# Delta rule in chunks: the odd heads on exchanged halves of the rows, and the last scan piece between the two halves of the per-chunk products

## The reference

```python
H, CHUNK = 4, 64
h = silu(causal_conv4(x));  q, k = l2norm(h @ Wq), l2norm(h @ Wk);  v = h @ Wv   # per head
beta = sigmoid(h @ Wb);  g = h @ Wg
def step(S, xs):                       # over the chunks of one head
    qc, kc, vc, bc = xs
    kb = kc * bc[:, None]
    A = jnp.tril(kb @ kc.T, -1)
    U = solve_triangular(eye + A, vc * bc[:, None] - kb @ S, lower=True)
    o = qc @ S + jnp.tril(qc @ kc.T) @ U
    return (S + kc.T @ U, o)
out = (rms_norm(o) * norm_w * silu(g)) @ Wo
```

## Time and profile before

| | us |
|---|---|
| median of 3 runs (823.71 to 824.50) | 824.07 |
| span of the profiled execution | 869.1 |
| in it: until the delta stage | 113.6 |
| in it: delta stage, steps 2 to 15 | 144.3 |
| in it: what follows the delta stage | 579.8 |

### The profile page before, as it was taken

The page is one execution under the profiler, slowest core; times in us unless marked ns, Lnnn a source line. Parts: engine busy times, 40 slices in busy tenths (PEclk is TensorE's granted clock), DMA queues, the critical chain, the costliest instruction groups (busy, mean ns, idle before and its releaser), DMA issues. The chain is left out here.

```text
span 869.1 us, 38511 instructions
## 1 busy us (share of the span) xinstructions
PE 638.0 (73%) x15559; PEld 550.7 (63%) x15559; DVE 388.2 (45%) x1166; ACT 275.3 (32%) x666; POOL 375.3 (43%) x773
## 2 busy tenths in 40 slices
PE   5775457888888585616998368889985269989993
PEld 4564346888888484516988335567664158978992
DVE  3664602222222135661666413445762844456662
ACT  4552211111111121404665133434532023334441
POOL 4574554211110372055888473220100444387675
PEclk9796655555555566856999757889997569999997
DMA  4001231131110470064655110000000556555551
GB/s 124 8 15 32 69 91 40 59 97 49 54 49 34 142 225 1 0 105 144 196 181 171 40 43 23 16 15 4 4 4 2 91 140 203 191 182 184 198 192 38
DMA packets 64818, 75.08 MB, mean 86 GB/s; under 512 B 16048, under 2 KB 42704, under 8 KB 64704
## 3 DMA queue, kind: packets, MB, share of 16 engines
q1 hardware_dynamic: 60384, 64.38, 24.1%
q0 software_dynamic: 4320, 9.18, 4.4%
HBM read 19.83 MB, written 11.24 MB: 36 GB/s over the span
## 5 line engine op out<-in xcount | busy, mean ns | idle before, releaser
L2017 PE MATMUL e_psH<-spare,e_up_w 128*128 x728 | 102.2, 284 | 9.7 <-issue 6.2
L2017 PEld LDWEIGHTS e_psH<-spare,e_up_w 128*128 128x128 f32 x728 | 90.1, 195 | 18.1 <-issue 18.1
L586 POOL TENSOR_TENSOR tb<-tinv,mb 128x128 f32<-128x128 f32 x64 | 24.3, 403 | 116.3 <-PE d_psY L606 110.1
L2082 ACT ACTIVATE e_pre<-e_psH 128x256 f32<-128x256 f32 x91 | 34.6, 382 | 71.1 <-PE e_psH L2017 66.6
L2027 PE MATMUL e_psY<-vb,e_hT 128*128 x364 | 56.0, 276 | 0.2
L1345 ACT ACTIVATE e_hT<-e_psH,e_b 128x128 f32<-128x128 f32 x156 | 44.6, 368 | 27.9 <-PE e_psH L1301 20.1
L2190 DVE SCALAR_TENSOR_TENSOR e_row<-e_psY,e_row 128x128 f32 x91 | 32.0, 351 | 47.9 <-issue 35.8
L1249 POOL DMA_INDIRECT e_row<-xe_dram,e_read_at x39 | 42.8, 1099 | 17.3 <-issue 6.8
L2183 DVE TENSOR_TENSOR e_hT<-e_pre,e_psH 128x256 f32<-128x256 f32 x91 | 37.6, 413 | 25.3 <-ACT e_pre L2082 15.2
L2027 PEld LDWEIGHTS e_psY<-vb,e_hT 128*128 128x128 f32 x364 | 47.9, 192 | 1.0 <-issue 0.9
L1733 DVE TENSOR_TENSOR spare<-l_psA,l_tri 128x512 f32<-128x512 f32 x64 | 39.7, 680 | 14.3 <-PE l_psA L1561 11.8
(11 more groups left out here) (348 smaller groups left out, 1643.4 us busy)
## 6 DMA issues: line engine op xcount, KB each, us to landing
e_up_w<-wac SPq DMA_DIRECT2D x91, 256.0 KB
e_up_w<-wa SPq DMA_DIRECT2D x39, 256.0 KB
xe_dram<-xe SPq DMA_DIRECT2D x2, 2192.0 KB, 15.4
vk_now<-vk SPq DMA_DIRECT2D x16, 192.0 KB, 2.1
kq_now<-kq SPq DMA_DIRECT2D x16, 192.0 KB, 2.3
outs_dram<-spare SPq DMA_DIRECT2D x39, 64.0 KB
r<-in_L_attn_hidden_states SPq DMA_DIRECT2D x8, 256.0 KB, 4.0
gk_now<-gk SPq DMA_DIRECT2D x16, 128.0 KB, 2.1
```

What stands on the lines that cost most here:

```text
L2017: mm = nc.tensor.matmul(psH[i % 3][:, f], up_w[i % WDEEP][:, f * P:(f + 1) * P], xT[:, bass.ds(t, 1)].rearrange("p a l -> p (a l)"), start ...
L2082: act.activation(pre[i % 2][:, :, :], psH[i % 3][:, 0:NF], ACT.Silu).then_inc(silu, 1)
```

## The change

Three things.

1. *Place.* Chunk c of an even head stays on rows 32c. Chunk c of an odd head is put on the rows of chunk (c + 2) mod 4 in everything that lies between `first` and the per-chunk products (`place(c, h)`; sums modulo 4 below). In `first` and `second` the odd heads use tile (c, c+2) and in `across` (c+2, c), where the even ones use (c, c); in the per-chunk products they use (c+2, h) for (c, h). The results go to two banks of `psY`, one for the even and one for the odd heads, with `across` in the second part of the same banks (`psZ` is gone).
2. *Order of the per-chunk products.* For each sequence b one kind of product goes over all heads and chunks (16 products on 16 tiles) before the next kind; `scan(t-1, 3)`, which stood ahead of all of them, stands between b = 0 and b = 1.
3. *What the stage before has to supply.* `gk` and `kq` must hold the odd heads on exchanged rows. The scores of odd heads are written there. GpSimd still needs K K^T of every head on its own rows, so 4 more products a block of 32 columns make that for the odd head of a pair, and 4 of 16 columns, against the identity, bring its keys to the exchanged rows. ScalarE copies these to a new `gu` (two copies) and into `kq` (one) after `gk`; `gk`'s semaphore `g_sb` becomes `u_sb` and is raised by the last of the three, and for pair 0 `gu` waits until GpSimd has read the group before. The copy of keys from `kqn` keeps the even heads alone. Two constants move into `spare`.

The core of the diff (before line numbers):

```diff
+def place(c, h):
+
+    return (c + 2 * (h % 2)) % NC
...
-                    pool.wait_ge(g_sb, 2 * g + 2)
-                    pool.tensor_tensor(ga[:, :, :, :], steps_of(gk, g)[:, :, :, 0:SUB], spread(mb[:, s, :, 0], SUB), ALU.mult).then_inc(a_step, 1)
+                    pool.wait_ge(u_sb, 2 * g + 2)
+                    pool.tensor_tensor(ga[:, :, :, :], gu[:, :, :, 0:SUB], spread(mb[:, s, :, 0], SUB), ALU.mult).then_inc(a_step, 1)
...
                         for c in range(NC):
                             for i in range(2):
+                                at = place(c, i) * CH
-                                mm = nc.tensor.matmul(psF[c * CH:(c + 1) * CH, i, k * 2 * CH:(k + 1) * 2 * CH],
+                                mm = nc.tensor.matmul(psF[at:at + CH, i, k * 2 * CH:(k + 1) * 2 * CH],
...
+                        for c in range(NC):
+                            at = 4 * 2 * CH + k * 2 * CH
+                            mm = nc.tensor.matmul(psF[c * CH:(c + 1) * CH, 1, at:at + CH],
+                                                  kqT[rows, n, 0, c * CH:(c + 1) * CH], kqT[rows, n, 0, c * CH:(c + 1) * CH],
+                                                  start=True, stop=True)
+                        for c in range(NC):
+                            at, to = 4 * 2 * CH + k * 2 * CH + CH, place(c, 1) * CH
+                            mm = nc.tensor.matmul(psF[to:to + CH, 1, at:at + DK],
+                                                  kqT[rows, n, 0, c * CH:(c + 1) * CH], eye[rows, 0:DK],
+                                                  start=True, stop=True)
...
-                                   ACT.Copy).then_inc(g_sb, 1)
+                                   ACT.Copy)
+                    if g and pair == 0:
+                        act.wait_ge(a_step, 2 * g)
+                    own_rows = psF[:, :, :].rearrange("p i (u k a l) -> p k i u a l", u=2, k=4, a=2)
+                    for i in range(2):
+                        act.activation(gu[:, :, 2 * pair + i], own_rows[:, :, i, i, 0], ACT.Copy)
+                    act.activation(steps_of(kq, g)[:, :, 2 * pair + 1, 0:DK], own_rows[:, :, 1, 1, 1, 0:DK], ACT.Copy).then_inc(u_sb, 1)
...
-                    dve.wait_ge(g_sb, 2 * g + pair + 1)
+                    dve.wait_ge(u_sb, 2 * g + pair + 1)
...
-        psY, psZ = bank("d_psY", [P, B * H, RW]), bank("d_psZ", [P, B * H, RW])
+        psY = bank("d_psY", [P, 2, 512])
...
-                            mm = nc.tensor.matmul(out[row(c), bh], tb[i][:, bh // H, bh % H].rearrange("p s i -> p (s i)")[row(c)],
+                            mm = nc.tensor.matmul(psY[row(place(c, bh)), bh % 2, y_of(bh)], tb[i][:, bh // H, bh % H].rearrange("p s i -> p (s i)")[row(c)],
...
-                            mm = nc.tensor.matmul(psZ[row(c), bh], gk_now[key(c), bh], y0[key(c), bh * RW:(bh + 1) * RW], start=True, stop=True)
+                            at = key(place(c, bh))
+                            mm = nc.tensor.matmul(psY[row(c), bh % 2, z_of(bh)], gk_now[at, bh], y0[at, seat(bh):seat(bh) + RW], start=True, stop=True)
...
+                def per_chunk(b, last):
+
+                    for h in range(H):
+                        bh, at = b * H + h, seat(b * H + h)
+                        for c in range(NC):
+                            on_row = row(place(c, h))
+                            nc.tensor.matmul(psC[row(h), c, b * P:b * P + RW], uw[on_row, at + DV:at + DV + CH], kq_now[on_row, bh],
+                                             start=True, stop=True)
...
                     scan(t - 1, 2)
+                    open_chunk(t, False)
+                    per_chunk(0, False)
                     scan(t - 1, 3)
-                    per_chunk(t, False)
+                    per_chunk(1, True)
```

More of the change, by code:

```diff
@@ L309, in scores @@
                     if 2 * g + pair:
-                        pe.wait_ge(g_sb, 2 * g + pair)
+                        pe.wait_ge(u_sb, 2 * g + pair)
                         pe.wait_ge(m_sb, 2 * g + pair)
@@ L601, in _, with apply @@
             def _(pe):
-                def apply(i, right, out, done):
+                def apply(i, right, done):
                     for bh in range(B * H):
                         for c in range(NC):
-                            mm = nc.tensor.matmul(out[row(c), bh], tb[i][:, bh // H, bh % H].rearrange("p s i -> p (s i)")[row(c)],
+                            mm = nc.tensor.matmul(psY[row(place(c, bh)), bh % 2, y_of(bh)], tb[i][:, bh // H, bh % H].rearrange("p s i -> p (s i)")[row(c)],
                                                   right(bh)[row(c)], start=True, stop=True)
@@ L615, in first @@
                     pe.sem_inc(passed, 1)
-                    apply(0, lambda bh: vk_now[:, bh], psY, y_ps)
+                    apply(0, lambda bh: vk_now[:, bh], y_ps)
                 def across(t, start):
@@ L631, in second, with open_chunk @@
                     pe.sem_inc(passed, 1)
-                    apply(1, lambda bh: zz[:, bh * RW:(bh + 1) * RW], psY, w_ps)
-                def per_chunk(t, start):
+                    apply(1, lambda bh: zz[:, seat(bh):seat(bh) + RW], w_ps)
+                def open_chunk(t, start):
                     if not start:
@@ L655, in per_chunk @@
-                    mm.then_inc(c_ps, 1)
+                def per_chunk(b, last):
[5 more added lines that the diff above has]
+                                             start=True, stop=True)
+                    for h in range(H):
+                        bh, at = b * H + h, seat(b * H + h)
+                        for c in range(NC):
+                            on_row = row(place(c, h))
+                            nc.tensor.matmul(psC[row(h), c, b * P + RW + CH:b * P + RW + 2 * CH], uw[on_row, at:at + DV], kq_now[on_row, bh, DK:RW],
+                                             start=True, stop=True)
+                    for h in range(H):
+                        bh, at = b * H + h, seat(b * H + h)
+                        for c in range(NC):
+                            on_row = row(place(c, h))
+                            mm = nc.tensor.matmul(psC[row(h), c, b * P + RW:b * P + RW + CH], kq_now[on_row, bh, 0:CH], uw[on_row, at:at + DV],
+                                                  start=True, stop=True)
+                    if last:
+                        mm.then_inc(c_ps, 1)
@@ L698, in _ @@
                         act.wait_ge(uw_done, t)
-                    act.activation(wide(y0), psY[:, :, :], ACT.Copy).then_inc(y_sb, 1)
+                    act.activation(wide(y0), psY[:, :, 0:HALF_W], ACT.Copy).then_inc(y_sb, 1)
                     act.wait_ge(z_ps, t + 1)
-                    act.activation(wide(zz), psZ[:, :, :], ACT.Copy, scale=mask_s[:, 1:2]).then_inc(z_sb, 1)
+                    act.activation(wide(zz), psY[:, :, HALF_W:2 * HALF_W], ACT.Copy, scale=mask_s[:, 1:2]).then_inc(z_sb, 1)
                     act.wait_ge(c_ps, t + 1)
```

40 lines of the change are left out of this document (20 added, 20 removed).

## The result

| | before | after |
|---|---|---|
| median | 824.29 us (823.71 to 829.61) | 842.50 us (838.40 to 845.43) |
| ratio | | 1.0205, interval 1.0154 to 1.0257 |

The prediction was 796.6 us (785 to 812) with 4% for slower. It was wrong in sign. Two steps of it failed. One is what the stage ahead pays: 17.6 us and not 2.7. The other is the clock at which the kernel before runs its delta stage: set against an execution near the median, that stage gains 0.5 to 2.6 us and not 30.

The account below looks back on a forecast made before the run. It took a single chain in each delta step, with TensorE at half clock, as the bound. Steps -30.7, step 0 -1.0 and the stage before +2.7 gave -29.0, scaled to -27.5: 796.6 us, range 785 to 812.

Parts of the forecast that it names:

- The three batches: Delta stage, `first`, `across` and `second` on eight tiles: from 1.50 to 1.02 us each, 1.44 us less a step.
- The fit: TensorE batch time, from the scores batch at two clocks: fixed 0.52 us plus 0.66 us going with columns over clock.
- Rival 4: Delta stage: two tiles of one row group take turns, batches stay at 1.5 us; 825 to 838 us, chance 6%.
- The per-chunk products: Delta step, 192 instructions over sixteen tiles: from 2.59 to 2.14 us, or 1.7; 0.75 less with scan piece 3's move.
- scan piece 3: Delta step, piece moved between the products' halves so the first waits only for uw; alone 0.13 us less a step.
- Rival 1: Delta stage: per-chunk products get no faster, above 3.2 us from uw to `on`; 805 us, chance 13%.
- The scaling by 0.948: Whole kernel: the sum of -29.0 us in the 869.1 us profile, scaled to the 824.07 us median, gives -27.5.
- Rival 2: Delta stage of the changed kernel: the clock rises to 2.4 GHz as work gets denser; about 785 us, chance 8%.
- The project stage: Stage before the delta stage: added products and copies make it end later, +2.7 us (1 to 8).
- The products' price: Project stage, 32 added products in each of sixteen scores batches: 0.6 us a batch at 1.2 GHz.
- The hiding: Project stage: of 16.8 us "if nothing hid it", most is hidden, leaving 1.2 in group 7 and 1.5 in the tail.
- Rival 3: Project stage pays in full: 16.8 us exposed, or 28 us of instruction traffic; 810 to 820 us, chance 7%.

Follow-up runs that it names:

- experiment 7: Changed delta stage with the project stage of the kernel before, plus idle TensorE products in the delta stage: 813.8 us, ratio 0.9847.
- Experiment 4: The changed kernel with scan piece 3 put back ahead of both halves of the per-chunk products: 840.6 us, ratio 1.0188 to the kernel before.
- experiment 2: The changed delta stage alone, with the project stage of the kernel before: 822.8 us, ratio 0.9969.
- experiment 5: The changed kernel without the 32 added products a scores batch, added copies kept: 824.2 us, ratio 0.9986.
- experiment 6: The changed kernel without the three added ScalarE copies, added products kept: 833.2 us, ratio 1.0096.
- experiment 9: The changed kernel with three large products a scores batch in place of the 32 added small ones: 839.5 us, ratio 1.0121.
- experiment 13: The changed kernel with two large products a scores batch in place of the 32 added small ones: 837.5 us, ratio 1.0156.
- experiment 14: The changed kernel with each added small product cut to 2 columns, same number of instructions: 839.7 us, ratio 1.0183.
- experiment 1: The kernel before run once more, no edit: 831.6 us, ratio 1.0024.
- experiment 3: The changed project stage alone, with the delta stage of the kernel before: 846.9 us, ratio 1.0235.
- experiment 12: The kernel before run again, no edit, for a trace near the median: 824.66 us, trace span 822.9.
- experiment 8: The kernel before with idle TensorE products added behind scan pieces and at the end of a pass in its delta stage: 817.8 us, ratio 0.9914.
- experiment 10: The changed kernel with idle TensorE products added in its delta stage: 842.7 us (828.9 to 861.5), ratio 1.0036, unclear.

## Why the prediction was wrong, point by point

*The three batches* were right: 1.02 us forecast, 1.01 measured. The fit also held at full clock (0.77 forecast for the new layout, 0.80 measured in experiment 7). What I did not ask is what the old layout takes there: 0.88. The new one is worth 0.49 us a batch at 1.2 GHz and 0.08 at 2.4. Rival 4, with batches left at 1.5, is refuted. The Trainium skill's rule named there (TensorE: Matmul & The Clock Gate, Part 3: Packing small matmuls) is that weight loads overlap running matmuls only in another row group. These batches do not show it: they use two tiles of each row group and take 1.01 us, not 1.50.

*The per-chunk products* and *scan piece 3* were mis-sized. Experiment 4 shows the products' new order worth 0.31 us where 0.45 or more was forecast (2.59 to 2.14 or 1.7), and the piece's move worth nothing where 0.13 was: it saves 0.49 us of waiting instead of 0.60 and costs 0.52 instead of 0.47. From uw to `on` the step gained 0.28 us and not 0.75. Rival 1 did not come true: its sign was more than 3.2 us there, and it is 3.11. A step lost 1.8 us instead of 2.19: a size, not the sign.

*The scaling by 0.948* is the first step that failed. I saw 869.1 us against a median of 824, wrote that I could not see which stages hold the difference, and spread it evenly. More than half of it lay in the very stage that the change is about: at the median the kernel before takes 150.1 us there and not 174.1. The -31.7 us for steps were -24.5 against the first trace and -0.5 against one near the median. The view that speaks of it was the earlier trace rows: a stage at 0.5 among others with 7 to 9. I took that clock for a property of the stage; it was one of that execution.

*Rival 2* asked about the clock and looked for its rise in the wrong kernel: the old layout was granted more than half, the new one was not. In the eight traces with the new layout and no idle products (after, experiments 2, 4, 5, 6, 9, 13, 14) it was 0.50 in every step; in the old layout it was 0.50, 0.50 and then 0.79, 0.75, and 0.80 (before, experiments 1, 3 and 12). The new layout does the same work in less of TensorE's time, and in experiments 7 and 8 the fuller engine got the clock in either layout. The share of busy time alone does not decide it: 86% at 0.50 in the earlier trace rows, 84% at 0.50 in experiment 2, 80% at 0.80 in experiment 12, and 100% at 0.50 for 63 us in experiment 10. That the shorter batches are what keeps the clock down fits the runs without idle products, but no run changes them alone; the cause stays open.

*The project stage* is the second step that failed: +2.7 forecast, +17.6 measured. The products' price was 0.60 us a batch at full clock and 0.84 at half, against the 0.6 forecast for half; the copies' was right (0.46, from 118.52 to 118.98, against 0.45). The hiding was wrong. I looked for slack link by link, and found it for the squares and the reduction, but not on VectorE's queue: 14 of the 16 masks wait for the last copy, and kqn and the convolution of the next group wait behind the mask. By the split above, some 6.8 us of the products' 9.6 came through and 3.0 of the copies' 7.2. TensorE's stops, which the sum had at nothing, are 7.0 more. That these add up to 16.8, the figure of "if nothing hid it", is chance.

Rival 3 (7%) had both parts, and its sign, a start later by over 12 us, is what the trace shows. It priced the program at the whole of step 1, 28 us; by what step 1 takes above a later step, 14.20 - 10.31 = 3.89 us for 256 products, it would have been 7.8, an estimate that lies near the 7.0. Rival 3 still ended at 810 to 820, because it kept the delta stage's full gain. Without that gain, lost to the clock of the kernel before, the change is slower.

## What to carry to other kernels

Before costing an edit, hold the profiled span against the timed runs; if they differ by more than the edit is worth, find the stage that holds the difference before taking any duration from it, above all where TensorE's clock is 0.5. An edit that shortens TensorE's bursts in a chain of short waits may earn nothing if the longer bursts had the full clock. And work added ahead of a wait has to be costed by what is queued behind the waiting instruction, and not only by what that instruction itself can spare.

## What the runs showed of the hardware

- One program was granted 0.50 and 0.80 of the clock in the same steps in two executions, and its delta stage took 174.1 and 150.1 us.
- Idle products shortened the kernel before by 0.9%: TensorE 97% busy, clock 0.95. Yet in another kernel TensorE was busy for all of 63 us at 0.50.
- Small products cost by number: 64 of them (128 instructions) hold TensorE for 1.45 us at full clock whether half of them have 16 to 32 columns or 2.
- With many small products in straight-line code TensorE stopped four times in the middle of a batch, for 1.1 to 2.3 us, 7.0 in the project stage; with few large ones never. Each stop ended 1.20 to 1.60 us after a packet of instructions had arrived.
